# Packing the adjacency two tiles ahead: the order of TensorE's work in one step of a graph attention kernel

## The reference: what is computed

```python
h = maximum(layernorm(x), 0)
support = (h @ weight).reshape(-1, 4, 64)              # per head
f1 = einsum(support, weight_u);  f2 = einsum(support, weight_v)
scores = leaky_relu(f1[j] + f2[i], 0.2) * adj[i, j]    # masked where it is 0
attn = softmax of the row over its non-zero entries
out = x + attn @ support + bias + h @ proj_w.T + proj_b
```

## Time and profile before

| | |
|---|---|
| median of 3 runs | 862.98 us (861.75 to 863.88) |
| the profiled execution | 860.12 us, of which the span of the trace is 858.4 us |
| TensorE busy | 710.9 us (83%), mean granted clock 0.889 of full |
| VectorE busy | 643.1 us (75%) |
| GpSimd busy | 529.0 us (62%) |
| ScalarE busy | 129.3 us (15%) |
| HBM read and written | 328.99 MB and 16.91 MB, 403 GB/s over the span |

### The profile page before, as it was taken

How to read it: one execution, slowest core, us unless ns; L and a number is a source line. 1 busy time by engine, 2 the same in 40 slices (tenths; PEclk the granted TensorE clock), 3 DMA queues, 4 the chain that set the end, 5 groups by cost and what they waited for, 6 DMA issues and landing times.

```text
span 858.4 us, 11157 instructions
## 1 busy us (share of the span) xinstructions
PE 710.9 (83%) x3011; PEld 434.2 (51%) x3011; DVE 643.1 (75%) x2740; ACT 129.3 (15%) x467; POOL 529.0 (62%) x598
## 2 busy tenths in 40 slices
PE   2989999999956878887888888788888878888865
PEld 0656666666513545454555445354544445454454
DVE  4556666657446988879869798977979787886887
ACT  0223333333210111000001011000011100000010
POOL 4344455454467776667766667676766766676570
PEclk9999999999966989888879898887989888988789
DMA  9999999999999999999999999999999999999971
GB/s 307 422 407 393 416 422 416 407 423 413 419 410 384 385 401 402 388 405 384 402 393 374 399 374 405 383 404 384 390 396 375 406 366 400 359 403 401 397 302 53
DMA packets 63855, 329.82 MB, mean 384 GB/s; under 512 B 12795, under 2 KB 15560, under 8 KB 31024
## 3 DMA queue, kind: packets, MB, share of 16 engines
q1 hardware_dynamic: 43056, 286.28, 83.8%
q0 software_dynamic: 18432, 34.30, 11.1%
q10 hardware_dynamic: 2304, 8.52, 2.4%
HBM read 328.99 MB, written 16.91 MB: 403 GB/s over the span
## 4 chain that ended last, share of the span: by engine, by line
PE 42%; DMA 25%; DVE 24%; issue 4%; POOL 3%; ACT 1%; POOLq 0%; ACTq 0%; SPq 0%
DMA adj_raw<-in_adj 21%; PE ps_words L400 11%; PE ps_agg L461 9%; PE ps_agg L381 7%; PE ps_two L381 6%; DVE att L933 5%; PE ps_two L400 5%; DVE cand L787 3%; DVE base L943 3%; POOL att L717 2%; DMA att<-support_table,idx 2%; PE ps_score L445 2%; DMA att<-in_x 1%; PE ps_words L392 1%; DMA support_table<-att 1%
## 5 line engine op out<-in xcount | busy, mean ns | idle before, releaser
L717 POOL DMA_INDIRECT att<-support_table,idx x384 | 417.4, 1087 | 188.7 <-issue 105.8
L400 PE MATMUL ps_words<-adj_raw,pack_w 128*128 128x512 fp8e4 x640 | 186.7, 428 | 25.4 <-DMA adj_raw<-in_adj 25.3
L461 PE MATMUL ps_agg<-att,ident 128*128 128x260 f32 x640 | 176.3, 428 | 8.5 <-DVE att L933 8.5
L461 PEld LDWEIGHTS ps_agg<-att,ident 128*128 128x128 f32 x640 | 135.1, 218 | 41.6 <-issue 18.6
L400 PE MATMUL ps_two<-adj_raw,pack_w 128*128 128x512 fp8e4 x384 | 118.9, 457 | 24.6 <-DMA adj_raw<-in_adj 24.5
L400 PEld LDWEIGHTS ps_words<-adj_raw,pack_w 128*128 128x128 bf16 x640 | 62.1, 106 | 125.3 <-DMA adj_raw<-in_adj 39.8
L787 DVE MAX8 cand<-ps_words 128x8 f32<-128x128 f32 x320 | 67.1, 281 | 66.3 <-PE ps_words L400 66.3
L933 DVE TENSOR_TENSOR att<-att 128x1536 f32<-128x1536 f32 x64 | 109.4, 1750 | 0.4 <-ACT att L625 0.4
L708 POOL COPY record<-att 128x8 f32<-128x8 f32 x64 | 13.4, 209 | 117.4 <-ACT att L569 117.4
L400 PEld LDWEIGHTS ps_two<-adj_raw,pack_w 128*128 128x128 bf16 x384 | 38.7, 113 | 91.5 <-DMA adj_raw<-in_adj 40.0
L381 PE MATMUL ps_agg<-w_all,hT 128*128 128x260 f32 x256 | 63.0, 389 | 4.1 <-ACT hT L565 4.1
(11 more groups left out here) (118 smaller groups left out, 821.2 us busy)
## 6 DMA issues: line engine op xcount, KB each, us to landing
adj_raw<-in_adj SPq DMA_DIRECT2D x256, 1024.0 KB, 13.3
support_table<-att ACTq DMA_DIRECT2D x16, 520.0 KB, 8.8
att<-in_x SPq DMA_DIRECT2D x16, 512.0 KB, 6.7
out<-base SPq DMA_DIRECT2D x15, 512.0 KB, 14.1
att<-support_table,idx POOLq DMA_INDIRECT x384, 6.2
out<-base SPq DMA_DIRECT2D x4, 128.0 KB, 1.9
w_all<-in_proj_wT SPq DMA_DIRECT2D x2, 128.0 KB, 6.0
w_all<-in_weight SPq DMA_DIRECT2D x2, 128.0 KB, 6.3
```

The lines of the kernel that those rows point to most:

```text
L400: mm = nc.tensor.matmul(ps_words[buffer_of(t)][:, k * 512:(k + 1) * 512], pack_w[:, u * UT + s, :], adj_low[:, n % HELD, s, k * 512:(k + 1 ...
L461: mm = nc.tensor.matmul(ps_agg[:, b, 0:ROW], ident[:] if k < OWN else onehotT[:, g % RING, b], gathered[:, g % RING, b, k], start=(k == 0) ...
L717: pool.indirect_dma_start(gathered[:, g % RING, b, k, :], None, table, bass.IndirectOffsetOnAxis(idx[:, g % RING, b, k:k + 1], 0), bounds_ ...
```

## The change

`offsets(g)` stays first in TensorE's step. Behind it now comes everything that VectorE's step waits for (both aggregations, the records, the row scores, the references), and then the packs of the step in one go. They are of tile t + 2 for each tile t picked in the step, where they were of t + 1; tile 17 (`FIRST + 1`) is packed ahead of the loop. The written-out end, from `offsets(LATE)` on, stays as it is, and so do the programs of the other engines. The loads and their buffers are the same.

```diff
             pe.wait_ge(s_staged, TILES)
+            pack_places(FIRST + 1)
+            for u in range(UNITS):
+                pack_unit(FIRST + 1, u)
             for g in range(LATE):
-                new = [t + 1 for t in picks[g]]
                 offsets(g)
-                pack_places(new[0])
-                for u in range(UNITS // 2):
-                    pack_unit(new[0], u)
                 if g >= 2:
                     aggregate(g - 2, 0)
                 edge_records(g)
                 if g > 0:
                     row_scores(g - 1)
-                for u in range(UNITS // 2, UNITS):
-                    pack_unit(new[0], u)
-                if g > 0:
-                    edge_refs(g - 1)
                 if g >= 2:
                     aggregate(g - 2, 1)
-                for t in new[1:]:
-                    pack_places(t)
-                    for u in range(UNITS):
-                        pack_unit(t, u)
+                if g > 0:
+                    edge_refs(g - 1)
+                for t in picks[g]:
+                    if t + 2 < TILES - 1:
+                        pack_places(t + 2)
+                        for u in range(UNITS):
+                            pack_unit(t + 2, u)
```

More of the change, by code:

```diff
@@ L476, in _ @@
                     row_scores(g - 1)
-                for u in range(UNITS // 2, UNITS):
-                    pack_unit(new[0], u)
+                if g >= 2:
+                    aggregate(g - 2, 1)
                 if g > 0:
                     edge_refs(g - 1)
-                if g >= 2:
-                    aggregate(g - 2, 1)
-                for t in new[1:]:
-                    pack_places(t)
-                    for u in range(UNITS):
-                        pack_unit(t, u)
+                for t in picks[g]:
[3 more added lines that the diff above has]
+                            pack_unit(t + 2, u)
             offsets(LATE)
```

## The result

The changed kernel takes 867.67 us (median of 7 runs, 865.78 to 869.11) against 862.98 us (7 runs, 858.91 to 863.88) on the same chip: 4.7 us more, ratio 1.0063 with a 95% interval of 1.0046 to 1.0080. Medians are over a kernel's fast runs; only e4 had slow ones, two of six over 1.5% above its fastest, and they are left out. The profiled execution took 867.67 us, its span is 865.9 us; that of the kernel before, 860.12 us, was 2.9 us quicker than its median. The instruction count is the same, 11157. Lines behind the change have numbers lower by one (L867 is L866 now).

A forecast was written before the change was run, and what follows sets the result against it. The adjacency stream on the DMA engines was taken as the bound. Steady state 0, start 0 and end +4.5 us on the profiled 860.12 gave 864.6; with 2.9 for the median, 867.5 us, range 860 to 880.

The forecast's parts named there:

- The stream does not care: Steady state: the adjacency stream sets the pair at 38.3 us, loads get buffers in time; change costs 0.
- T: Steady state: the end of a two-tile pack, where TensorE has caught up with the stream; later times count from it.
- the first release: Two-pick step: first buffer handed back after the chain work, claimed at T + 25.9 to T + 27 us.
- the eleventh load: Each pair: load needing the late-released buffer, claimed issued 6.2 to 7.3 us ahead of its due landing.
- The point at which B decides: Each pair: first release later than T + 28, 1.9 us before the tenth landing, makes loads run dry.
- B: Loads run dry at each pair's eleventh unit: 1 us per pair, 14 pairs, 881.5 us in all; chance 0.17.
- The end: Steps 29 and 30: VectorE later against the stream, +3.0 to +4.6 us, +6.5 with low clock; taken as +4.5.
- The lag: Written-out end: VectorE's L867 of step 30 moves from 815.78 to 819.1 to 819.9, +3.3 to +4.1 us.
- 0.5 plain or 2.5 with the low clock: References of step 30: row scores start with L867, +0.5 us; the low clock adds about 2 us.
- A: Steps 28 and 29: VectorE's waits shrink, so the lag misses the end; +1.5 us, 864.5; chance 0.20 with D.
- C: Stream: DMA dips were the cost and go; half the 18 us gain less the end, 858.5 us; chance 0.14.
- D: Loop: packs wait for the same buffer's pick, so nothing runs ahead; 863 us; counted with A, chance 0.20.

The follow-up runs named there:

- e4: Changed kernel with packs one tile ahead instead of two, chain work still first: 985.4 us, 1.1325 times the kernel before.
- e7: Changed kernel with 49 extra matmuls, results unused, in TensorE's waits behind the loop: 861.25 us, 0.9995 times the kernel before.
- e5: Changed kernel with one buffer fewer, five loads in flight instead of six: 898.77 us, 1.0426 times the kernel before.
- e10: Changed kernel itself, unaltered, on one more chip where the kernel before took 873.12 us: 910.8 us, 1.0430 times.
- e6: Kernel before with one buffer fewer, five loads in flight instead of six: 863.9 us, 1.0020 times the kernel before.
- e13: Kernel before with extra matmuls, results unused, in TensorE's waits behind the loop: 870.69 us, 0.9967 times the kernel before.

## Why the prediction was right, and where it was not

The forecast was 867.5 us, measured 867.67; +4.5 us against +4.7.

*The stream does not care.* Right on the chip of the result: last landing 3.3 us earlier, not later, though the queue was almost empty in 8 of the 14 pairs. VectorE's two-pick step started at 615.52, T + 14.8 (forecast T + 16.0), the first release came at T + 27.6 with the issue (T + 25.9 to 27), and the eleventh load landed within 5.1 us of it (6.2 to 7.3), in those 8 pairs 5.0 to 5.6 us, and not so late in the others. e7, with the same loop, records that load's landings, and two of them have still less:

```profile
L317 SPq DMA_DIRECT2D adj_raw<-in_adj x1: 328/328/328, 399.9 to 399.9; - x1
DMA to landing us min/median/max: 4.8/4.8/4.8
```

Its stream ended at 811.5 us all the same. So the mechanism held with less room than forecast. The term of 0 for the stream was in truth -3.3 us in the trace; most of that lead is there by 352 us, and what made it no run shows.

*The point at which B decides.* It was put at T + 28, 1.9 us before the tenth landing. The changed kernel stood at T + 27.6 and lost nothing; e5 moved the edge by one unit and lost 37 us against before; in e10 the issue came at T + 29.9 and B was there, 38 us where I had priced 14 for 14 pairs and 18.5 with the end. What the prediction had wrong for that chip is a term that it put at nothing: it took SyncE's issue to follow the end of the unit's matmuls at once. It does on the chip of the result (0.03 us); in the eight pairs of e10 it came 1.57 to 4.67 us later, since TensorE's signal was late. The bound of 1.9 us from an issue to flowing data held (data flowed within a microsecond in the changed kernel). That I gave B 0.17 is fair for the chip at hand and too little for chips in general.

*The end.* The lag was computed at 3.3 to 4.1 us and is 4.0 (4.9 less 0.9 behind the last landing). It did not show as such, since the stream was early; what showed is 0.8 us at L866, 2.3 us more at the references (2.94 us of wait against 0.67), forecast as 0.5 plain or 2.5 with the low clock. The Trainium skill, "TensorE: Matmul & The Clock Gate", section "HAM oscillation — how this bites in real kernels", has batches behind long waits start at the low clock; this trace agrees: after a wait of 3.01 us for one_hot the aggregation took 4.13 us, against 2.44 before. Not foreseen is that the last 25 us may run at the low clock too, 4.5 us in this trace. Since e6 shows it without the change, both orders can end so; that the change makes it more frequent would fit 4.7 us in the median, but with one trace a kernel that is argued, not shown. Shown is that e7, which keeps the clock up, is level with before.

*A, C, D.* C is out: the dips grew deeper and e6 lost nothing with fewer loads. D is out: VectorE's waits for words did go. A fell in the result and describes e7.

The forecast's total is thus right, its place too (behind the stream), and its lag was sized well. That the total came out to 0.2 us is luck: in the traces it is made up of -3.3 us in the stream (forecast 0), +4.0 lag, +2.3 at the references (forecast 0.5 in the sum) and +4.5 behind them (forecast 0), which is 7.5; 2.9 of these are the quick execution of before, and the medians show 4.7. How those 4.7 us divide between lag and clock is open.

## What to carry to other kernels

When work that hands back buffers is moved, compute for the latest release of a period how long before its due landing the new load is issued, and keep a whole load of reserve: some 5 us were enough on one chip, and on another the same program lost 38 us. Do not test on one chip a change that uses up a queue's reserve. Behind the last transfer, where engines wait for each other in turn, a few idle-time matmuls are worth trying: they brought the changed kernel level and made the kernel before 0.3% faster (e13, 870.69 against 873.12 us, 0.9938 to 0.9997 times).

## What the hardware did that I had not expected

- TensorE's signals arrived late on two of the chips: SyncE issued 1.10 us after the start of a pack in the changed kernel and in e7, 2.65 to 5.74 us in eight pairs of e10, and a result for VectorE came 5.9 us after its end, where 0.04 us is usual. The kernel before took 861.73 us on a chip without them, 871.16 and 873.12 us on these two.
- The landing pace held at 3.2 us a unit through stretches in which the engines moved 89 GB/s for a microsecond: 8.8 us of missing share in 396 us cost nothing.
- The same aggregation took 2.44 or 4.67 us at the end in executions whose TensorE code is equal (before and e6), and the stretch from L867 of step 30 on took 42.6 or 49.1 us.
